# A score offset moved from TensorE to GpSimd and VectorE, and the order of two small products

## The reference

```
cq = einsum('bcd,bqd,d->bcq', c, q, w_cq) + b_cq
s = (c @ w_c + b_c)[:, :, None] + (q @ w_q + b_q)[:, None, :] + cq
a = softmax(s, axis=2)
c2q_att = einsum('bcq,bqd->bcd', a, q)
b_att = softmax(max(s, axis=2), axis=1)
q2c_att = einsum('bc,bcd->bd', b_att, c)[:, None, :]
x = concatenate([c, c2q_att, c * c2q_att, c * q2c_att], axis=-1)
z = x @ W_l.T + b_l
```

## Time and profile before

| What | Value |
|---|---|
| Median of 3 runs | 1377.8 us |
| The profiled execution | 1374.36 us |
| Its span (first to last instruction) | 1372.4 us |
| Busy in the span | TensorE 94%, its loads 83%, VectorE 72%, ScalarE 57%, GpSimd 38% |
| Granted TensorE clock, mean | 0.976 |

### The profile page before, as it was taken

The page is one execution under the profiler, slowest core; times in us unless marked ns, Lnnn a source line. Parts: engine busy times, 40 slices in busy tenths (PEclk is TensorE's granted clock), DMA queues, the critical chain, the costliest instruction groups (busy, mean ns, idle before and its releaser), DMA issues.

```text
span 1372.4 us, 41789 instructions
## 1 busy us (share of the span) xinstructions
PE 1290.7 (94%) x16144; PEld 1136.1 (83%) x16145; DVE 986.1 (72%) x2428; ACT 780.1 (57%) x1482; POOL 517.5 (38%) x557
## 2 busy tenths in 40 slices
PE   4899999996999999988999999999999999999976
PEld 3788888875999999976788888888888888888866
DVE  3688888866655555537788788878877887788673
ACT  3455556642655555546656665666666666666632
POOL 2266666654122222247344324432443344332000
PEclk9899999998899999999999999999999999999988
DMA  3123242211422222221110111011101110110000
GB/s 104 45 74 128 76 137 78 76 68 64 137 76 77 76 77 77 65 77 39 29 33 13 31 35 33 14 31 35 33 14 29 37 31 15 29 37 14 8 4 16
DMA packets 86510, 71.06 MB, mean 52 GB/s; under 512 B 25072, under 2 KB 73200, under 8 KB 86352
## 3 DMA queue, kind: packets, MB, share of 16 engines
q1 hardware_dynamic: 74752, 42.71, 10.9%
q0 software_dynamic: 11600, 26.10, 6.0%
HBM read 40.73 MB, written 28.05 MB: 50 GB/s over the span
## 4 chain that ended last, share of the span: by engine, by line
PE 39%; DVE 10%; issue 3%; ACT 2%; POOL 1%; DMA 0%; DVEq 0%; POOLq 0%; ACTq 0%
PE c_ps_w L83 17%; PE c_ps_w L1566 7%; PE c_ps_w L1583 4%; PE c_ps_s L1532 4%; PE c_ps_w L1555 3%; PE c_ps_w L1541 3%; DVE c_r_max L1944 2%; DVE c_shifted L1942 2%; DVE c_shifted L1945 2%; PE c_ps_w L1463 1%; DVE c_probs L1957 1%; DVE c_xn_t_low L1867 1%; DVE k_ctx_t_low L898 1%; ACT c_o_t L1747 1%; ACT c_q_t L1719 1%
## 5 line engine op out<-in xcount | busy, mean ns | idle before, releaser
L1376 POOL TENSOR_TENSOR c_rstd<-c_var,c_minus_half 128x1 f32<-128x1 f32 x64 | 35.7, 558 | 353.7 <-DVE c_var L1925 353.6
L92 POOL DMA_INDIRECT sorted_x<-a_xn,f_slot_of x128 | 128.4, 1003 | 92.4 <-PE a_ps_w L767 36.0
L1566 PEld LDWEIGHTS c_ps_w<-c_wo,c_o_t 128*128 128x128 f32 x1024 | 125.1, 196 | 33.9 <-ACT c_o_t L1747 27.1
L1566 PE MATMUL c_ps_w<-c_wo,c_o_t 128*128 128x128 f32 x1024 | 130.9, 282 | 20.7 <-ACT c_o_t L1747 20.6
L1350 POOL DMA_INDIRECT c_back<-sorted_y,k_y_row_of x112 | 110.9, 991 | 102.2 <-PE c_ps_w L1555 52.9
L1109 PE MATMUL d_ps_y<-e_w_all,d_h_t 128*128 x1136 | 138.7, 276 | 0.0
L1109 PEld LDWEIGHTS d_ps_y<-e_w_all,d_h_t 128*128 128x128 f32 x1136 | 133.6, 193 | 0.0
L980 POOL DMA_DIRECT2D sorted_y<-d_y_rows x71 | 50.8, 716 | 208.6 <-DVE d_y_rows L1011 204.3
L1942 DVE TENSOR_TENSOR c_shifted<-c_ps_s,c_mask 128x1024 f32<-128x1024 f32 x64 | 78.3, 1224 | 57.8 <-PE c_ps_s L1532 57.7
L1719 ACT ACTIVATE c_q_t<-c_ps_w 128x512 f32<-128x512 f32 x120 | 70.2, 602 | 85.7 <-PE c_ps_w L83 84.7
L1058 ACT ACTIVATE d_h_t<-d_ps_h,d_biases 128x256 f32<-128x256 f32 x284 | 112.0, 476 | 2.5 <-PE d_ps_h L83 2.0
(11 more groups left out here) (250 smaller groups left out, 3554.7 us busy)
## 6 DMA issues: line engine op xcount, KB each, us to landing
d_x_rows<-sorted_x SPq DMA_DIRECT2D x71, 128.0 KB, 2.1
sorted_y<-d_y_rows POOLq DMA_DIRECT2D x71, 128.0 KB, 2.2
k_X<-in_x SPq DMA_DIRECT2D x16, 256.0 KB, 3.0
a_q_rows<-in_ctx SPq DMA_DIRECT2D x16, 256.0 KB, 3.3
ctx_cols<-a_q_t SPq DMA_DIRECT2D x16, 256.0 KB, 2.0
k_ctx_raw<-ctx_cols SPq DMA_DIRECT2D x16, 256.0 KB, 2.8
out<-k_X SPq DMA_DIRECT2D x16, 256.0 KB, 3.1
sorted_x<-a_xn,f_slot_of POOLq DMA_INDIRECT x128, 2.2
```

The costliest lines, as they stand in the source:

```text
L92: pool.indirect_dma_start(out=sorted_x, out_offset=bass.IndirectOffsetOnAxis(ap=slot_of[:, choice, t:t + 1], axis=0), in_=xn2[:, k, :], in ...
L1566: last = pe.matmul(w[:, 0:D], o_t[:, j, :], wo[:, j, :], start=(j == 0), stop=(j == J - 1))
```

## The change

The offset of a row is computed in another place. GpSimd multiplies the normalised rows `c_rows` by w_c, now held as a row of 128 numbers in each partition (`weigh_context`, 128x512), and VectorE sums each of the four tiles' 128 products (`sum_context`). Both are done for group t + 1 in turn t. The four one-column products on TensorE are gone, and `s_max` reads `c_offset` from SBUF. Two new semaphores order these steps.

Apart from that the sums of the counts stand behind both halves of the down product, in `filled()` and in TensorE's loop, and VectorE adds the second half before it places the tiles in the turn of the last group.

```diff
--- before.py
+++ after.py
@@ -102,7 +102,8 @@
     BANKS, AHEAD, KEPT = 8, 3, 4
     with ExitStack() as ctx:
         m = Space(nc, ctx, "a")
-        w_cq, w_q, w_c = m.sb("w_cq", [P, 1]), m.sb("w_q", [P, 1]), m.sb("w_c", [P, 1])
+        w_cq, w_q, w_c = m.sb("w_cq", [P, 1]), m.sb("w_q", [P, 1]), m.sb("w_c", [P, D])
+        c_weighted, c_offset = m.sb("c_weighted", [P, GT, D]), [m.sb(f"c_offset{i}", [P, GT]) for i in range(2)]
         biases = m.sb("biases", [P, 3])
         bias_sum = m.sb("bias_sum", [P, 1])
         b_l = m.sb("b_l", [P, D])
@@ -165,6 +166,7 @@
         b_shifted, b_exped, batt_ready, bdiag_ready = m.sem("b_shifted"), m.sem("b_exped"), m.sem("batt_ready"), m.sem("bdiag_ready")
         x_offset, z_added, xt_ready, logits_ready = m.sem("x_offset"), m.sem("z_added"), m.sem("xt_ready"), m.sem("logits_ready")
         h_ready, x_added = m.sem("h_ready"), m.sem("x_added")
+        c_weighted_ready, c_offset_ready = m.sem("c_weighted_ready"), m.sem("c_offset_ready")
         route_constants, counts_ready, base_ready, slots_ready = (m.sem(n) for n in ("route_constants", "counts_ready", "base_ready", "slots_ready"))
         experts_loaded, cleared = m.sem("experts_loaded"), m.sem("cleared")
         totals_read, tails_ready, tails_filled = m.sem("totals_read"), m.sem("tails_ready"), m.sem("tails_filled")
@@ -197,12 +199,12 @@
                     yield ("down", d, 0)
                 if a is not None:
                     yield ("s", a)
+                if d is not None:
+                    yield ("down", d, 1)
                 if c is not None:
                     yield ("sums", c)
                 if c == G - 1:
                     yield ("totals", 0)
-                if d is not None:
-                    yield ("down", d, 1)
                 if a is not None:
                     yield ("mrow", a)
                 if b is not None:
@@ -246,7 +248,7 @@
             load(0)
             sp.dma_start(w_cq[:], column(T["L0_xattn_w_cq"])).then_inc(w_loaded, 16)
             sp.dma_start(w_q[:], column(T["L0_xattn_w_q"])).then_inc(w_loaded, 16)
-            sp.dma_start(w_c[:], column(T["L0_xattn_w_c"])).then_inc(w_loaded, 16)
+            sp.dma_start(w_c[:], T["L0_xattn_w_c"].partition_broadcast(P)).then_inc(w_loaded, 16)
             for n, name in enumerate(("L0_xattn_b_cq", "L0_xattn_b_c", "L0_xattn_b_q")):
                 sp.dma_start(biases[:, n:n + 1], T[name].partition_broadcast(P)).then_inc(w_loaded, 16)
             sp.dma_start(b_l[:], T["L0_xattn_b_l"].partition_broadcast(P)).then_inc(w_loaded, 16)
@@ -344,6 +346,13 @@
                 x_g = X[:, GT * g:GT * (g + 1), :]
                 pool.tensor_tensor(x_g, x_g, b_l[:].unsqueeze(1).to_broadcast([P, GT, D]), ALU.add).then_inc(x_offset, 1)
 
+            def weigh_context(g):
+
+                if g > 0:
+                    pool.wait_ge(c_offset_ready, g)
+                pool.wait_ge(cnorm_ready, GT * (g + 1))
+                pool.tensor_tensor(c_weighted[:], c_rows[g % 2][:], w_c[:].unsqueeze(1).to_broadcast([P, GT, D]), ALU.mult).then_inc(c_weighted_ready, 1)
+
             def scatter(g, first, last):
                 pool.wait_ge(xnorm_ready, GT * (g + 1))
                 pool.wait_ge(slots_ready, g + 1)
@@ -359,6 +368,7 @@
             pool.wait_ge(shared_loaded, 64)
             root1(1)
             offset_x(0)
+            weigh_context(0)
             for t in range(TURNS):
                 a, b, c, d = groups_of(t)
                 if d is not None and d < G - 1:
@@ -379,6 +389,8 @@
                     scatter(c, 1, 2)
                 if b is not None:
                     root2(b)
+                if t + 1 < G:
+                    weigh_context(t + 1)
                 if c is not None:
                     scatter(c, 2, 3)
                     if a is not None:
@@ -597,6 +609,10 @@
                 b2 = w1_all[:, :, HC * P + HC:]
                 step(dve.tensor_tensor(b2, b2, bs2[:].unsqueeze(1).to_broadcast([P, E, D]), ALU.add))
 
+            def sum_context(g):
+                dve.wait_ge(c_weighted_ready, g + 1)
+                dve.tensor_reduce(c_offset[g % 2][:], c_weighted[:], AX.X, ALU.add).then_inc(c_offset_ready, 1)
+
             def shift_scores(g):
                 if g >= 1:
                     dve.wait_ge(s_exp, g)
@@ -605,7 +621,8 @@
                 s_view = bank("s", g)[:, 0:GT * S].rearrange("p (k q) -> p k q", q=S)
                 step(dve.tensor_reduce(row_max[:], s_view, AX.X, ALU.max))
                 dve.tensor_tensor(scores[:], s_view, row_max[:].unsqueeze(2).to_broadcast([P, GT, S]), ALU.subtract).then_inc(s_shifted, 1)
-                dve.scalar_tensor_tensor(s_max[:], bank("s", g)[:, GT * S:GT * S + GT], bias_sum[:, 0:1], row_max[:],
+                dve.wait_ge(c_offset_ready, g + 1)
+                dve.scalar_tensor_tensor(s_max[:], c_offset[g % 2][:], bias_sum[:, 0:1], row_max[:],
                                          ALU.add, ALU.add).then_inc(smax_ready, 1)
 
             def shift_batches(g):
@@ -685,6 +702,7 @@
             statistics1(0)
             norm_shift1(0)
             statistics1(1)
+            sum_context(0)
             for t in range(TURNS):
                 a, b, c, d = groups_of(t)
                 if c == G - 1:
@@ -701,6 +719,7 @@
                 if c is not None:
                     slots(c)
                 if c == G - 1:
+                    add_shared(d, 1)
                     place_tiles()
                     compare_choices()
                     place_rows()
@@ -708,7 +727,7 @@
                     shift_batches(a)
                     attention_weights(a)
                     batch_weights(a)
-                if d is not None:
+                if d is not None and c != G - 1:
                     add_shared(d, 1)
                 if b is not None:
                     add_z(b)
@@ -720,6 +739,8 @@
                     normalise2(b)
                 if a is not None:
                     weighted(a)
+                if t + 1 < G:
+                    sum_context(t + 1)
                 if t + 2 < G:
                     statistics1(t + 2)
             weigh_choices()
@@ -750,9 +771,6 @@
 
             def make_scores(g):
                 w = begin("s", g)
-                pe.wait_ge(ct_ready, 3 * g + 1)
-                for k in range(GT):
-                    pe.matmul(w[:, GT * S + k:GT * S + k + 1], c_t[g % 2][:, k * P:(k + 1) * P], w_c[:, 0:1], start=True, stop=True)
                 pe.wait_ge(ct_ready, 3 * g + 3)
                 for k in range(GT):
                     for b in range(NB):
@@ -856,12 +874,12 @@
                     feed_down(d, 0)
                 if a is not None:
                     make_scores(a)
+                if d is not None:
+                    feed_down(d, 1)
                 if c is not None:
                     sum_counts(c)
                 if c == G - 1:
                     sum_totals()
-                if d is not None:
-                    feed_down(d, 1)
                 if a is not None:
                     transpose_maxima(a)
                 if b is not None:
```

## The result

| | before | after |
|---|---|---|
| timed runs, median (lowest to highest), us | 1378.11 (1377.33 to 1380.77), 6 runs | 1384.31 (1383.03 to 1385.46), 6 runs |
| the same kernels again on another occasion, us | 1378.81 (1376.61 to 1383.23), 25 runs | 1384.93 (1382.51 to 1386.65), 12 runs |
| profiled execution, us | 1374.36 | 1385.22 |
| steady turn of the first stage, us | 17.78 | 18.52 |
| granted clock of the whole | 0.976 | 0.977 |

The change makes the kernel slower by 0.4%: ratio 1.0040, 95% interval 1.0027 to 1.0053, and the second time 1.0038, 1.0025 to 1.0051. The forecast was 1396 us, +18.5; measured are +6.2 us. The direction was right and the size three times too large.

The account below looks back on a forecast made before the run. TensorE set the 17.78 us turn, VectorE close behind; VectorE would then bound it at 19.22. Twelve steady turns +17.3, opening +1.4 and end -0.2 gave +18.5, on the median 1377.8 about 1396 us, range 1383 to 1409.

Parts of the forecast that it names:

- VectorE becomes the bound: First stage: VectorE's turn, 16.93 us without its waits for TensorE, grows to 17.54 with the sum, against TensorE's 16.83.
- Place 1: GpSimd's weighing starts 0.14 us before VectorE's second normalisation and holds the first of four: 0.89 us per turn.
- The sum, 0.61: VectorE's added sum of 128x512 to 128x4 costs 0.61 us per turn, between 0.42 and 1.22.
- Place 2: GpSimd's bias addition comes 0.35 us ahead of VectorE's b_att and holds it: 0.79 us per turn.
- Rival A: Only place 1 holds, as z or GpSimd's scatter comes later and b_att goes first: +9, 1387 us; chance 23%.
- TensorE's order at price 0: Sums of the counts behind the second down half on TensorE: no new wait, 0 to 0.3 us per turn.
- The opening: First stage's turns 0 to 2: later row maximum, place 1 and the sum, together +1.4 us, between 0 and +3.
- The end: Turn 16 gains 3.3 us as its counts' wait goes, turn 17 loses 3.1: -0.2, between -3.5 and +0.5.
- The base: The +18.5 us, worked out on the profiled 1374.36 us, was added to the timed median of 1377.8 us.
- Rival D: The forecast plus a falling clock in steady turns as TensorE idles: 1405 to 1430 us; chance 15%.

Follow-up runs that it names:

- experiment 1: The changed kernel with GpSimd's weighing moved directly behind the bias addition, ahead of the scatters and the second root: 1374.8 us, ratio to before 0.9951.
- experiment 10: The kernel of experiment 1, word for word, timed again beside new runs of before on one chip: 1373.84 us, ratio 0.9959.
- experiment 5: The kernel before, word for word, run again for a second profile: 1378.11 us, ratio 1.0003.
- experiment 3: The kernel before with only the sums of the counts and the totals moved behind the whole down product: 1383.82 us, ratio 1.0010.
- experiment 4: The changed kernel with the sums of the counts put back between the two down halves: 1407.28 us, ratio to before 1.0182.
- experiment 12: The kernel of experiment 1 with the sums of the counts back between the down halves in every turn: 1397.85 us, ratio to before 1.0132.
- experiment 7: The changed kernel with VectorE's addition of the second shared half put ahead of b_att: 1398.52 us, ratio to before 1.0152.
- experiment 8: The kernel before without the one-column products and with nothing in their place, sums still between the down halves: 1378.05 us, ratio 0.9997.
- experiment 9: The kernel before with GpSimd's second scatter waiting for the scores' end, not the first down half's: 1378.91 us, ratio 0.9996.

## Why the prediction was right in direction and wrong in size

**VectorE becomes the bound: right.** Its waits for the logits are gone, and of those for the row maximum 0.2 us are left. Its turn without collisions was put at 17.54 us and is 17.63. What is left as a gain without place 1 is real and small: experiments 1 and 10.

**The sum, 0.61: right**, 0.60 in the trace.

**Place 1, 0.89: right.** 18.52 - 17.62 = 0.90, and taking the weighing away from there gives it back. By the rule of the Trainium skill ("SBUF — State Buffer", section "Who interferes with whom") the engine that issues first keeps the port; the trace agrees, with the weighing 0.15 us ahead at 177.39 and the first normalisation at 1.19 us in place of 0.34.

**Place 2, 0.79: the step that failed.** The prediction put the bias addition at 5.12 us after the row maximum, "3.94 us" behind the maxima's transpose as before. It starts at 5.66 (173.27 - 167.61), b_att at 5.54. The transpose came where it was put (168.76, +1.15). But the addition waits for two things: z, and the four tiles of `c_rows` from ScalarE (`offset_x` waits for `cnorm_ready`). The working looked at z alone. ScalarE's rows, before and after:

```profile
165.78 1.63 ACT L401 ACTIVATE a_c_rows<-k_X,a_shift,a_rstd 128x128 f32<-128x128 f32 x4
```
```profile
171.27 0.31 ACT L437 ACTIVATE a_b_exp<-a_b_shift 4x128 f32<-4x128 f32 x1 [1.00 <-DVE a_b_shift L634]
171.49 1.63 ACT L413 ACTIVATE a_c_rows<-k_X,a_shift,a_rstd 128x128 f32<-128x128 f32 x4
```

They end at 167.41 and at 173.12. Counted from the row maximum that is 5.44 and 5.51: they stand behind b_att's exponential, which waits for VectorE, so they hang on VectorE's chain, and a TensorE that comes earlier hardly moves them. Before, z ended last and hid them; the profile of before had the row. With them the addition could not have come before 5.5, that is a few hundredths behind b_att at 5.47 and not 0.35 ahead. z itself came later behind the transpose too, and it is z that ends the addition's wait: the addition starts 4.51 us behind the transpose and not 3.94. Its last product starts 0.2 us later than the working has it (4.93 us after the row maximum), and the addition 0.7 to 0.8 us after that product and not 0.38, the late report of experiment 5. So the margin by which b_att comes first, 0.12 to 0.19 us, rests in part on something that stays open. This step holds 12 x 0.79 = 9.5 of the 12.3 us that the forecast was too high. Rival A, with 23%, is what happened; it named a late z, but not the rows.

**TensorE's order at price 0: right for the order alone** (experiment 3), **and misread for the whole.** Neither the sum nor a rival gave the order a worth of its own. Experiments 4 and 12 put a price on it: without the new order the move of the offset costs 20 us more ((1.0182 - 1.0040) x 1378), and 24 us with the weighing out of the way, with TensorE waiting 1.7 to 1.9 us for the counts, ready work behind it. Of the two parts of the change the order is the one that makes the other bearable. The prediction's row (no wait at 179.53) was true only as long as the one-column products filled 0.95 us ahead of it.

**The opening, +1.4; measured +1.83**, at turn 3's row maximum (74.89 - 73.06). **The end, -0.2; measured +0.6**, from turn 15's row maximum (+9.62) to the last scatter (345.82 - 335.58 = +10.24). Turn 16 did give the 3.3 us: z's reader comes 7.76 us behind the logits and not 11.09. It gave 2.4 of them back at once: a scatter of GpSimd stands ahead of the second root, the normalisations wait, and the clock falls all the same: TensorE is idle for 2.09 us before the transposes of xn, and the granted clock, 1.00 up to 323 us, is 0.50 from 325 to 329.

```profile
320.84 0.97 POOL L92 DMA_INDIRECT sorted_x<-a_xn,f_slot_of  x1 [1.93 <-issue]
321.83 1.04 POOL L341 TENSOR_TENSOR a_rstd<-a_var,a_minus_half 128x4 f32<-128x4 f32 x1
...
323.01 1.12 DVE L680 TENSOR_SCALAR a_xn<-k_X,a_mv,a_rstd 128x128 f32<-128x128 f32 x4 [2.72 <-POOL a_rstd L341]
```

Turn 17 lost 1.6 us (18.38 against 16.74 from the logits to the last scatter) where 3.1 were named. That the end came out within 0.8 us is luck: an error of 2.4 us and one of 1.5 nearly cancel.

**The base.** The sum was right to be made against the profiled execution, and wrong to be added to the median as it stood. That execution had turns of 17.78 us; another, at 1379.15 us, had 18.17, and the timed runs sit with the second. The changed kernel's turns are 18.52 in both of its profiles. So from row maximum 3 to 15 the change loses 221.16 - 213.37 = 7.8 us against the first profile, but only 221.16 - 217.99 = 3.2 against the second. It is in part luck that the 7.8 is also the 12 x 0.65 of rival A: eleven turns lose 0.75 each, and the twelfth, in which VectorE has no statistics of a next group to make, takes 17.35 us and gains 0.4. The tally: 18.5 less 9.5 for place 2 are 9.0, with 0.4 more in the opening, 0.8 in the end and 0.7 that the rows don't break down 10.9, the difference of the first two profiles; less 4.7, 6.2. Of the 4.7, 3.8 are what before's median stands above its first profiled execution (1378.11 - 1374.36), and 0.9 what the changed kernel's profiled execution stands above its own median (1385.22 - 1384.31).

**Rival D** fell: from 100 to 280 us the clock stayed at full speed, though TensorE was idle for 8 us of it (length and busy times as in experiment 4, the clock third from the end).

```profile
100.00:280.00 180.00, 172.17 (x1303) 141.17 (x1301) 157.64 (x592) 103.83 (x173) 129.63 (x118) 1.00 0.32 96
```

Its condition was not met in this kernel, whose longest idle piece is 0.8 us. But experiment 7 meets it, with pieces of 1.43 to 1.52 us in each turn, as long as turn 16's 1.46, and the clock stays at 1.00. So one idle piece of that length does not decide it, and the rival's rule was wrong as well. In experiments 4 and 12 it is 0.96 in the same stretch, with idle pieces of up to 1.9 and 1.7 us.

## What to carry to other kernels

When two engines run within a few per cent of each other, taking work from one buys only the slack of the other, and an instruction that waits must not stand in front of work that is ready: the same products removed changed the time by nothing, -6, +6 or +25 us, by what stood where (experiments 8, 10, the change, experiment 4). Before a step is moved earlier in a forecast, list every semaphore that it waits for; the wait that the profile names is the last one, and the others set how far it can move. A product on GpSimd was free beside VectorE's statistics and cost VectorE 0.85 us when it started 0.15 us ahead of the normalisations, so look for its place. And take a second profile of before: its turn was 17.78 us in one and 18.17 in the other.

## What the runs showed of the hardware

- Which engine starts first decides all of it. b_att 0.12 to 0.19 us ahead of the addition, in 11 turns of the changed kernel: 0.28 us, and the addition 1.26 to 1.30. b_att 0.16 behind it: 1.24 us. In turn 0 b_att starts 0.02 behind it and takes 1.39; in one turn of experiment 7 it starts 0.01 ahead, keeps 0.28, and the addition takes 1.41.
- The same program ran its first stage at two speeds in its two profiled executions, 17.78 and 18.17 us a turn, with the granted clock at full speed in both. In the slower one VectorE sees the end of the scores and of z 1.1 to 1.3 us after their last product's start, in the faster one after 0.37; experiment 9 shows it at z alone. A kernel in which VectorE arrives later than TensorE does not feel it: 17.63 and 17.62 us in two executions of experiment 1's kernel, 18.52 in both of the changed one.
- An idle piece of TensorE as long as one after which the clock fell does not by itself make it fall: 1.43 to 1.52 us in each turn of experiment 7, granted clock 1.00.
- In turn 16 GpSimd idled 1.93 us ahead of a scatter for nothing that the profile shows; it wasn't tried what that is.
